# Two cross-attention layers on one core: bfloat16 for the shift's product, sums' product behind the maxima's, prologue waits moved to their first use

## The reference, cut to what matters

```
h = layernorm(x) * gamma + beta;   Q = h @ Wq;  K = ctx @ Wk;  V = ctx @ Wv      # layer 0, 16 heads of 64
x = x + (softmax(Q K^T) * 64**-0.5 @ V) @ Wo + bo
xn = rmsnorm(x) * norm_w;  q = xn @ wq;  k, v = ctx @ wkv                        # layer 1, 16 heads of 32
q, k = l2norm(rope(q)), l2norm(rope(k))
x = x + (softmax(q k^T * sqrt(32)) @ v) @ wout
```

## Time and profile before

| | |
|---|---|
| median of 3 runs | 3244.57 us (3243.3 to 3245.17) |
| the profiled execution, its own time | 3240.73 us |
| its span in the profile | 3238.5 us |
| PE busy | 3054.9 us, 94% of the span |
| DVE busy | 2299.2 us, 71% |
| ACT busy | 1390.0 us, 43% |
| POOL busy | 484.6 us, 15% |
| mean granted TensorE clock | 0.991 of full speed |

### The profile page before, as it was taken

The page is one execution under the profiler, slowest core; times in us unless marked ns, Lnnn a source line. Parts: engine busy times, 40 slices in busy tenths (PEclk is TensorE's granted clock), DMA queues, the critical chain, the costliest instruction groups (busy, mean ns, idle before and its releaser), DMA issues.

```text
span 3238.5 us, 70505 instructions
## 1 busy us (share of the span) xinstructions
PE 3054.9 (94%) x30408; PEld 1596.4 (49%) x30408; DVE 2299.2 (71%) x2677; ACT 1390.0 (43%) x1472; POOL 484.6 (15%) x221
## 2 busy tenths in 40 slices
PE   5999998999899999899999999999999999999997
PEld 3554445554355445555445445455534445455552
DVE  3677777677777777678767777667866777776866
ACT  2333333556433333356643333335563333334564
POOL 1000001352000000236100000034400000013530
PEclk8999999999999999999999999999999999999999
DMA  3011010111111010011111010102012011110001
GB/s 112 13 26 28 21 26 16 53 28 41 46 52 25 23 27 20 18 58 30 38 46 50 23 28 22 26 15 61 24 39 74 22 25 25 23 25 20 21 17 37
DMA packets 178394, 107.10 MB, mean 33 GB/s; under 512 B 81452, under 2 KB 147116, under 8 KB 178088
## 3 DMA queue, kind: packets, MB, share of 16 engines
q1 hardware_dynamic: 178088, 102.60, 11.8%
HBM read 93.12 MB, written 9.42 MB: 32 GB/s over the span
## 4 chain that ended last, share of the span: by engine, by line
PE 81%; DVE 9%; issue 4%; ACT 3%; DMA 2%; SPq 1%; POOL 0%; DVEq 0%; ACTq 0%; POOLq 0%
PE scores L697 19%; PE o_acc L709 19%; PE work L736 12%; PE work L730 12%; PE work L779 10%; PE work L665 5%; DVE acc L881 4%; PE work L768 3%; ACT probs L809 2%; DVE tile_max L860 1%; PE work L772 1%; PE work L762 1%; DVE stats L901 1%; PE work L789 1%; DVE sumsq L942 1%
## 5 line engine op out<-in xcount | busy, mean ns | idle before, releaser
L809 ACT ACTIVATE probs<-scores 128x1024 f32<-128x1024 f32 (+1 forms) x768 | 982.0, 1310 | 515.6 <-PE scores L697 511.1
L860 DVE TENSOR_REDUCE tile_max<-work 128x2 f32<-128x1024 f32 x496 | 606.8, 1223 | 464.8 <-PE work L665 464.5
L881 DVE TENSOR_TENSOR acc<-acc,probs 128x1024 f32<-128x1024 f32 (+1 forms) x544 | 859.8, 1580 | 31.9 <-ACT probs L809 9.6
L709 PE MATMUL o_acc<-probs,v_tok 128*64 128x512 f32 (+1 forms) x4096 | 771.0, 607 | 0.2 <-ACT probs L809 0.2
L998 POOL TENSOR_TENSOR inv<-sumsq,power 128x16 f32<-128x16 f32 x64 | 186.2, 2909 | 1991.1 <-DVE sumsq L944 1991.1
L779 PE MATMUL work<-wo,o_sum 128*32 128x512 f32 (+1 forms) x2072 | 398.9, 599 | 41.6 <-issue 23.0
L697 PE MATMUL scores<-q_high,k_high 32*128 32x512 f32 (+1 forms) x2048 | 341.8, 450 | 16.0 <-ACT probs L809 14.1
L709 PEld LDWEIGHTS o_acc<-probs,v_tok 128*64 128x64 f32 (+1 forms) x4096 | 164.9, 122 | 331.6 <-issue 319.5
L966 DVE TENSOR_TENSOR resid<-work,resid 128x512 f32<-128x512 f32 x384 | 261.9, 686 | 76.8 <-PE work L779 74.6
L697 PE MATMUL scores<-q_low,k_high 32*128 32x512 f32 (+1 forms) x2048 | 311.7, 393 | 0.0
L697 PE MATMUL scores<-q_high,k_low 32*128 32x512 f32 (+1 forms) x2048 | 310.5, 393 | 0.0
(11 more groups left out here) (79 smaller groups left out, 2529.1 us busy)
## 6 DMA issues: line engine op xcount, KB each, us to landing
recip<-rows_dram SPq DMA_DIRECT2D x380, 64.0 KB, 2.1
stage<-in_x_dram SPq DMA_DIRECT2D x8, 1024.0 KB, 7.1
wq<-in_L_xattn_Wq_dram SPq DMA_DIRECT2D x32, 256.0 KB, 2.8
resid<-in_x_dram SPq DMA_DIRECT2D x8, 1024.0 KB, 5.2
wo<-in_L_xattn_Wo_dram SPq DMA_DIRECT2D x32, 256.0 KB, 2.7
out_dram<-resid SPq DMA_DIRECT2D x8, 1024.0 KB, 4.2
wk<-in_L_xattn_Wk_dram SPq DMA_DIRECT2D x32, 192.0 KB, 2.5
wv<-in_L_xattn_Wv_dram SPq DMA_DIRECT2D x32, 192.0 KB, 2.5
```

The lines of the kernel that those rows point to most:

```text
L709: mm = pe.matmul(o_acc[h * d:(h + 1) * d, :], v_tok[par][:, kt, h * d:(h + 1) * d], probs[:, unit_slot(t, n, kt, h // 2), h % 2, :], start ...
L809: act.activation(block_probs(t, n, kt), scores[:, 2 * (no % 2):2 * (no % 2) + g, :], ACT.Exp, scale=(1.0, float(D1) ** 0.5 / QK_SCALE ** 2 ...
L860: dve.tensor_reduce(tile_max[:, qt, :, n:n + 1], maxima_banks(e), AX.X, ALU.max, negate=True).then_inc(dve_freed, 1)
L881: dve.tensor_tensor(a, block_probs(t, n, 0) if kt == 1 else a, block_probs(t, n, kt), ALU.add).then_inc(add_ok, units)
```

## The change

It has three parts. The fourth product of the first layer's scores takes ones and `shift` in bfloat16 in place of fp32r (the negated maxima are bfloat16 parts in any case). In those steps whose beside entries begin with a `T`, the sums' product `den` of the half before is put behind `T` and no longer ahead of it. And three waits of the prologue go to the instruction that first needs what they wait for: DVE's for the tables, POOL's for the bias, ACT's for `affine`; ACT gets a small exponential of `power` as its first instruction.

```diff
-    beside[0][:0] = E("den", t, n)
+    at = 1 if beside[0] and beside[0][0].kind == "T" else 0
+    beside[0][at:at] = E("den", t, n)
...
-        ones_r = sb("ones_r", [P, P], F32R)
+        ones_b = sb("ones_b", [P, P], BF16)
...
-        shift = [sb(f"shift{i}", [P, S], F32R) for i in range(2)]
+        shift = [sb(f"shift{i}", [P, S], BF16) for i in range(2)]
...
-                        k_rows = ones_r[r, :] if kk is None else kk[r, tile(kt)]
+                        k_rows = ones_b[r, :] if kk is None else kk[r, tile(kt)]
...
+                    if (e.t, e.i) == ((0, 0), (0, 0)):
+                        act.wait_ge(affine_in, 16 * 3)
                     act.wait_ge(work_full, e.full)
...
-            act.wait_ge(affine_in, 16 * 3)
+            act.wait_ge(power_ok, 1)
+            act.activation(gate[:, 1:2], power[:, 0:1], ACT.Exp)
             run(lambda e: None, scored, attended, entry)
...
+                if no == 1:
+                    dve.wait_ge(tables_in, 16 * 2)
                 dve.wait_ge(squares_ok, no)
...
-            dve.memset(ones_r[:, :].bitcast(F32), 1.0)
+            dve.memset(ones_b[:, :], 1.0)
...
-            dve.wait_ge(tables_in, 16 * 2)
             run(rowmax, lambda t, n, kt: None, added, entry, on_vector)
...
                 if b == 0:
+                    pool.wait_ge(bias_in, 16)
                     pool.wait_ge(xn_ok, norm_no((0, 0), 1))
...
             pool.wait_ge(power_ok, 1)
-            pool.wait_ge(bias_in, 16)
```

## The result

The changed kernel takes 3194.04 us in the median of 5 runs (3187.79 to 3195.61), the kernel before 3244.57 us (3242.06 to 3246.38). The ratio is 0.9842, with a 95% interval of 0.9828 to 0.9855: 51 us less. The profiled execution took 3187.79 us, 52.9 us less than the profiled one of before; forecast were 53.5 from the same basis, and 3191 us for the median.

What follows compares the result with a forecast made beforehand. The prediction took PE to bound the kernel, 81% of the last-ending chain. Savings of 16.5 + 29 + 8 = 53.5 us from 3240.73 give 3187.2, plus 3.84 for the median: 3191 us, 8-in-10 range 3179 to 3205.

Steps and rivals of the forecast that it cites:

- the likeliest case: Whole kernel: the forecast as summed, 3191 us, own range 3183 to 3199, chance 0.57.
- prologue: Ahead of the first scores: idling 15.2, function table load 0.6, full clock 0.7, together 16.5 us less; bounds 13 to 19.
- order: `R` behind `T`: 0.64 us in 44 places, 0.54 in 4, less 1.3, about 29 us less; bounds 22 to 31.
- bfloat16: Shift's product in the first layer's scores: 512 pairs each 0.0175 us shorter, 9 us, taken as 8.
- the bound of 13: Prologue: 3.4 us come back if the query projection, 3.67 us at full clock, falls into a half-clock stretch.
- The term of 0.7 us: Prologue: the 16 transposes ahead of the query projection may run at full clock without the idling, 0.7 us less.
- the working had the copy of `T` set the time of `R`: Behind `T`: ACT's copy lets PE resume at 406.18; PE's own products would allow `R` at 406.16.
- The lost cover of the sums: Sums' way through DRAM ahead of `out`: 0.86 us later in PE's frame, cover falling from 1.9 to 1.0 us.
- the forecast has 1.3: One half a batch where DVE already waits for the sums' DMA: 1.3 us lost over four batches.
- 512 x 0.0175 = 9 us: Shift's product pairs in the scores: distance 0.215 us in bfloat16 in place of 0.2325, for 512 pairs.
- The sign that the prediction named: Score products: nine starts of pairs spanning 1.83 us in place of 1.86 would show the bfloat16 gain.
- The prediction's rival on the change of type: Scores: weight loads not prefetched across fp32r/bfloat16 changes, 0.09 us for each of 1024, +92 us, 3291 us; chance 0.04.

Runs made afterwards that it cites:

- the exchange of the banks: Changed kernel with `T` in bank 2 and `den` in bank 0 or 1: 3234.48 us, ratio 0.997 to the kernel before.
- half as many late loads: Changed kernel with shift's product first of the four in odd key tiles, bfloat16 products side by side: 3191.97 us, ratio 0.9837 to the kernel before.

## Why the prediction was right, and where it was not

The median of 3194 us lies 3 us above the 3191 forecast and inside the likeliest case's own range. The single parts, in us:

| part | forecast | changed kernel's trace | the part alone |
|---|---|---|---|
| prologue | 16.5 | 15.4 to the first scores | 17.5 |
| order | 29 | 0.65 a place, in 48 places | 29 |
| bfloat16 | 8 | 2.6 (512 x 0.005) | 3.6 |
| sum | 53.5 | 52.9 between the two traces | 50.1 |

The forecast comes so near because the two large parts were right; in the parts alone, what bfloat16 fell short (4.4 us) is partly made up by the prologue (1.0 more). In the middle column the three terms come to 49.2 (15.4 + 31.2 + 2.6). Most of the 3.7 that are missing from 52.9 can be chance: PE's waits for sums that land late come to 12.2 us in the trace of before and to 9.0 in this one, and among the other traces that differ in one or two of the parts they go from 8.7 to 13.2.

**Prologue: right.** DVE's first statistics, 8.0 forecast, came at 7.48; PE's `xt`, 17 to 18, at 18.27, ruled by the key projection and not by DVE. The missing 1.1 us is the key projection, which took 1.05 us longer to its end than in the trace of before, at a pace that is the half clock's by inference (above). The prediction looked for the half clock in the query projection, with 3.4 us as its price. The kernel with the prologue alone had it there in part, at 1.7 us, but the gain didn't fall to the bound of 13, as its key projection was 1.4 us shorter than that of before. The statement that POOL's wait left in place would take part of the gain was shown, at 9 to 11 us. The term of 0.7 us came out by luck. The query projection starts 4.0 us behind `xt` in place of 4.6, as forecast, but the transposes themselves save more, 1.36 us (1.20 + 1.09 in place of 3.65), and half of that goes to a wait that the working didn't have: between its two groups of eight PE stands 0.50 us for DVE's `k_low` (19.97), and it then waits 1.19 us for ACT's `hT` in place of 0.96.

**Order: right, in mechanism and size.** `R` at 1.19 us behind `T` was forecast to 0.01 us, and the exchange of the banks shows that the waited-for copy is the cause. One detail differs: the working had the copy of `T` set the time of `R`, by 0.02, and it is PE's own products (383.44 + 0.10 is ahead of 383.59). The lost cover of the sums was not used up. In the half where DVE waited for the DMA before, it still waits, as the timeline of the changed kernel has it (compare):

```profile
521.66 0.69 DVE L894 TENSOR_TENSOR o_sum<-o_sum,recip 128x512 f32<-128x512 f32 x1 [2.10 <-DMA recip<-rows_dram]
...
522.46 1.08 PE L780 MATMUL work<-wo,o_sum 128*64 128x512 f32 x4 [1.41 <-issue]
```

PE's wait there is 1.41 us against 1.20. In this half it is 1.01 to 1.20 in the three traces with the old order and 1.40 to 1.91 in the seven with the new. Over the four batches it grew from 5.96 to 6.94 us, 0.98 in all, where the forecast has 1.3. The other waits of this kind shrank at the same time, from 6.3 to 2.0 us, so in the whole nothing of that loss is to be seen.

**bfloat16: the right sign, a third of the size.** The failing step is "512 x 0.0175 = 9 us". The 0.215 us of a bfloat16 pair is right where all pairs are bfloat16 (0.216 in the kernel with all of them). The fault was to put it beside fp32r pairs unchanged. At each change from fp32r to bfloat16 the load of the new weights isn't taken ahead, and the four products save 0.005 to 0.010 us and not 0.0175. That the late load is what costs this is argued and not shown by itself: the two always go together, and half as many late loads gave back about 0.01 us a step. The sign that the prediction named, nine starts spanning 1.83 us, was not met either: two times 0.926 is 1.85. The prediction's rival on the change of type had this mechanism, with a price of 0.09 for each of 1024 changes. What stood against it, that the changes around `T` cost nothing, was read from fp32 neighbours. There the load is hidden indeed; PEld in the changed kernel, between `out` (its second pair from 381.98) and `T`, with 128 rows and 64 columns in both:

```profile
381.98 0.12 PEld L758 LDWEIGHTS work<-ident_b,neg_max 128*64 128x64 bf16 x2 [0.29 <-issue]
```

The load of 381.98 starts with the fp32 pair of that time, 0.42 ahead of `T`. After fp32r, going by the load of 384.64, it would have come only with `T` itself. So the row that the prediction took had the right type behind the change, bfloat16, and another one ahead of it, fp32 in place of fp32r. The price of the change is an estimated 0.0175 less 0.005 to 0.010, that is about 0.01 us in each of 512 places, 4 to 6 us in all. The Trainium skill's rule (TensorE: Matmul & The Clock Gate, section Weight-path perf modes), that the element's width doesn't matter to the array's pace, which the page states in speaking of fp8 against bfloat16, is not what the runs show between fp32r and bfloat16: 0.2325 against 0.216 us for the same 512 columns.

The difference between 53.5 and 51 is smaller than what single executions differ by (the changed kernel's runs span 7.8 us), so beyond the single parts it explains nothing.

## What to carry to other kernels

Where a short, regular wait stands in front of one product many times, ask which bank's copy it really waits for, and put the copy's product earlier and a long product behind it; here the order gave 29 us, with the sums' later landing already in it. Waits that stand at the start of an engine's program for things needed much later hold up the whole first chain, and must all be moved together: one left on POOL kept 9 to 11 us of 15 to 17. A product in a smaller type amid products of another type is priced by its changes of type as well, so convert neighbours together or put the converted ones side by side, and take the price from a row with the same types on both sides.

## What the runs showed of the hardware

- A pair of 64-row matmuls with 512 columns stands 0.2325 us apart in fp32r and 0.216 us in bfloat16 with bfloat16 neighbours.
- The first pair behind fp32 products with 128 rows is followed by the next after 0.34 us if both are fp32r, and after 0.23 if both are bfloat16 (383.59 to 383.93; 386.33 to 386.55).
- A bfloat16 weight load behind an fp32r product started only when that product had gone through (384.64 behind 384.40), in all 512 places; behind an fp32 product (of another shape) or a bfloat16 product it started with it (381.98; 386.99).
- The same prologue met the slow pace at different places in different executions: six matmul instructions took 2.82 us in one and 5.46 us in another. The row of the granted clock showed this from about 18 us on, and not ahead of that.
